# 41 expert blocks with a carried remainder instead of 46, and the out projection one state sooner

## The reference, cut to what matters

```python
x = hidden_states                                   # (4, 512, 128): 2048 tokens, 16 tiles of 128
r = x_n + mamba_block(rmsnorm(layernorm(x)))        # in proj, conv, scan over 16 states, out proj
logits = rmsnorm(r) @ router_w                      # 8 experts
top_w, sel = top_k(softmax(logits), 2)              # two experts for each token
for e in range(8):                                  # FFN = 512
    out += w_e[:, None] * (silu(h @ Wg[e]) * (h @ Wu[e]) @ Wd[e])
# then x += r + out, a gated FFN (384 hidden), attention (16 heads, causal), the same FFN again
```

## Time and profile before

| what | value |
|---|---|
| runs | 688.85 us median of three (685.72 to 689.6) |
| the profiled execution | 688.8 us, its span 687.0 us |
| PE busy | 570.7 us, 83% |
| DVE / ACT / POOL busy | 475.6 / 400.9 / 324.6 us |
| scan stage, first block transposed, block loop, attention | 0 to 276, 276, 278 to 440, 440 to 687 us of the span |
| block loop, mean of one | silu L1353 598 ns, gate times up L1766 688 ns, weights copy L1343 1048 ns |
| indirect DMAs on POOL, mean of one | put L907 976 ns, scatter L899 1008 ns |
| power on POOL, L871 | 1074 ns |

### The profile page before, as it was taken

How to read it: one execution, slowest core, us unless ns; L and a number is a source line. 1 busy time by engine, 2 the same in 40 slices (tenths; PEclk the granted TensorE clock), 3 DMA queues, 4 the chain that set the end, 5 groups by cost and what they waited for, 6 DMA issues and landing times.

```text
span 687.0 us, 11539 instructions
## 1 busy us (share of the span) xinstructions
PE 570.7 (83%) x3652; PEld 379.7 (55%) x3671; DVE 475.6 (69%) x1266; ACT 400.9 (58%) x666; POOL 324.6 (47%) x285
## 2 busy tenths in 40 slices
PE   2967899678677887889989999757799989988887
PEld 1423343224254564879989899625545545544466
DVE  4759997998789987536335653587777878886052
ACT  2677657756755776556756656314356556656731
POOL 5259988895996994225785324412011112112010
PEclk9979999899897999999999999957999999999999
DMA  5845455443755453201152003232003003000001
GB/s 142 305 167 159 150 186 154 143 129 109 241 183 160 142 135 100 68 16 36 54 133 86 20 17 105 68 100 58 9 25 87 10 20 92 4 3 3 1 16 47
DMA packets 49085, 63.32 MB, mean 92 GB/s; under 512 B 7570, under 2 KB 29090, under 8 KB 48770
## 3 DMA queue, kind: packets, MB, share of 16 engines
q1 hardware_dynamic: 43682, 56.65, 27.5%
q0 software_dynamic: 2496, 5.15, 2.1%
q10 hardware_dynamic: 2848, 0.78, 0.5%
HBM read 44.84 MB, written 9.52 MB: 79 GB/s over the span
## 4 chain that ended last, share of the span: by engine, by line
PE 36%; DVE 9%; issue 7%; ACT 4%; POOL 3%; DMA 1%; ACTq 1%; POOLq 0%; another core or an unknown queue 0%; DVEq 0%
PE ps L1792 33%; DVE arena L1712 3%; ACT arena L1296 2%; POOL moe_rows L899 1%; DVE stats L1383 1%; PE ps L2153 1%; DVE x L1647 1%; POOL moe_out L907 1%; DVE nb L1396 1%; ACT r L1296 1%; DMA moe_out<-arena,xT 1%; PE ps L2160 1%; ACT arena L1316 1%; ACT arena L1304 1%; ACTq L1286 1%
## 5 line engine op out<-in xcount | busy, mean ns | idle before, releaser
L1792 PE MATMUL ps<-arena 128*128 128x128 f32 (+11 forms) x2147 | 329.2, 329 | 42.9 <-DVE arena L1712 17.9
L1792 PEld LDWEIGHTS ps<-arena 128*128 128x128 f32 (+2 forms) x2166 | 209.0, 157 | 130.2 <-issue 59.3
L1574 DVE TENSOR_TENSOR_SCAN arena<-ps,arena 128x512 f32<-128x512 f32 x128 | 149.8, 1210 | 21.4 <-ACT ps L1225 15.2
L926 POOL TENSOR_TENSOR arena<-arena 128x1024 f32<-128x1024 f32 x64 | 127.9, 2016 | 25.5 <-DVE arena L1561 19.8
L1792 PE MATMUL ps<-arena,ident 128*128 128x512 f32 x216 | 109.5, 644 | 30.9 <-DVE arena L1586 30.8
L1712 DVE CUSTOM_DVE_ANT_0 arena<-ps,cmask 128x128 f32<-128x128 f32 (+3 forms) x256 | 111.5, 488 | 26.4 <-PE ps L1792 25.2
L1225 ACT ACTIVATE ps<-arena 128x512 f32<-128x512 f32 x128 | 87.4, 689 | 47.2 <-DVE arena L1574 45.5
L1792 PEld LDWEIGHTS ps<-arena,ident 128*128 128x128 f32 x216 | 42.4, 207 | 85.9 <-issue 44.2
L1296 ACT ACTIVATE arena<-ps 128x1024 f32<-128x1024 f32 (+3 forms) x86 | 57.0, 709 | 38.0 <-PE ps L1792 37.6
L907 POOL DMA_INDIRECT moe_out<-arena,xT x46 | 44.9, 976 | 66.5 <-DVE arena L1736 57.1
L1766 DVE TENSOR_TENSOR arena<-arena,ps 128x512 f32<-128x512 f32 x46 | 31.6, 688 | 57.1 <-PE ps L1792 43.6
(11 more groups left out here) (220 smaller groups left out, 700.3 us busy)
## 6 DMA issues: line engine op xcount, KB each, us to landing
arena<-bc_rows SPq DMA_DIRECT2D x118, 256.0 KB, 3.7
arena<-arena SPq DMA_DIRECT2D x64, 64.0 KB
arena<-arena SPq DMA_DIRECT2D x28, 128.0 KB, 2.4
moe_rows<-arena SPq DMA_DIRECT2D x2, 1495.0 KB, 11.8
arena<-moe_rows SPq DMA_DIRECT2D x8, 325.0 KB, 4.3
arena<-in_L_attn_a_Wg SPq DMA_DIRECT2D x8, 256.0 KB, 4.2
arena<-in_L_attn_a_Wu SPq DMA_DIRECT2D x8, 256.0 KB, 4.8
arena<-moe_out SPq DMA_DIRECT2D x4, 512.0 KB, 4.5
```

What stands on the lines that cost most here:

```text
L926: G.tensor_tensor(dBx[:, g % RING, :, :], dx[:, :, cs], bs[:, g % BS, :].unsqueeze(1).to_broadcast([P, CT, L]), ALU.mult).then_inc(s_dbx, 1)
L1574: V.tensor_tensor_scan(hst[:, g % STATES, e, :], bank(6 + e), dBx[:, g % RING, e, :], 0.0, ALU.mult, ALU.add).then_inc(s_scan, 1)
L1792: return T.matmul(o, l, rr, start=start, stop=stop)
```

## The change

The first half gets exactly 16 blocks and the second 25, so 41. Full blocks of each expert come first, then the experts with the largest remainders get one more until 16 are taken; what does not fit goes to one carry block for each of the eight experts, which are the first eight blocks of the second half (expert known beforehand), topped up with tokens of the second half. Outputs of blocks 0 to 23 are stored plainly by SP; outputs of blocks 16 to 40 are scattered by POOL; the first half's outputs are then gathered by 16 indirect DMAs on POOL. Core of the diff (shortened):

```diff
-        NBLK = TH * 2 + NE - 1
+        FIRST = 2 * TH
+        SECOND = (FIRST * P + LEFT + NE * (P - 1)) // P
+        NBLK = FIRST + SECOND
+        assert FIRST * P == 2 * L * HB and LEFT == 256 and SECOND == 25
-        CH = (0, 3, 8, 13, 18, NBLK)
+        CH = ((0, 3, 8, 12, FIRST), (0, 3, 10, 23, SECOND))
...
-   ... first_1 + 2: ("out_proj", 0, 0), 58: ("z", 1, 0), 61: ("z", 1, 1)}
+   ... first_1 + 1: ("out_proj", 0, 0), 58: ("z", 1, 0), 61: ("z", 1, 1)}
-   (30, 1): ("rows", 1, 0), (32, 0): ("abs", 1, 0), ... (34, 0): ("exp", 1, 0), (35, 0): ("log", 1, 0),
-   (36, 0): ("squares", 0, 0), (36, 1): ("squares", 1, 0), (38, 0): ("norm", 0, 0), (38, 1): ("norm", 1, 0),
-   (40, 1): ("input", 0, 0), (41, 0): ("input", 1, 0), (43, 0): ("logits", 0, 0), (45, 0): ("exps", 0, 0),
+   (29, 1): ("rows", 1, 0), (31, 0): ("abs", 1, 0), ... (33, 0): ("exp", 1, 0), (34, 0): ("log", 1, 0),
+   (36, 0): ("squares", 0, 0), (36, 1): ("squares", 0, 1), (37, 0): ("squares", 1, 0), (37, 1): ("squares", 1, 1),
+   (39, 0): ("norm", 0, 0), (39, 1): ("norm", 0, 1), (40, 0): ("norm", 1, 0), (40, 1): ("norm", 1, 1),
+   (41, 1): ("input", 0, 0), (42, 0): ("input", 1, 0), (47, 0): ("exps", 0, 0),
-        DELTA_AT = {4: 1, 30: 2, 36: 3}
+        DELTA_AT = {4: 1, 30: 2, 38: 3}
-   "power": first_1 + 6, "h2turn": first_1 + 7, "router": first_1 + 9,
-   "top_a": first_1 + 11, "top_b": first_1 + 13, "rank": first_1 + 14, "slots": first_1 + 15
+   "power": first_1 + 7, "h2turn": first_1 + 8, "router": first_1 + 10, "top": first_1 + 12,
+   "rank": first_1 + 13, "fill": first_1 + 14, "slots": first_1 + 16, "weights": first_1 + 19
-        SCATTER_FROM = first_1 + 16
+        SCATTER_FROM = first_1 + 17
...
-        in_moe = {0: [("h2norm",)], 2: [("h2turn", 1)], 3: [("route",)], 4: [("top_a",)], 5: [("top_b",)],
-                  6: [("rank",)], 7: [("slots",)], 8: [("add_r", 0)], ...
-                  1: [("h2turn", 0), ("targets", 0)], 22: [("targets", 1)],
-                  27: [("combine", 0), ...], 30: [("combine", 1), ...], ...
+        in_moe = {0: [("h2norm",), ("h2turn", 0)], 1: [("h2turn", 1)], 2: [("route",), ("top",)], 3: [("rank",), ("slots",)],
+                  6: [("exps",)], 8: [("weights",)], 10: [("add_r", 0)], ..., 18: [("targets",)],
+                  28: [("combine", 0), ("f_norm", 0, 0)], 29: [("f_normalise", 0, 0)], 30: [("f_turn", 0, 0), ("f_low", 0, 0)],
+                  33: [("combine", 1), ("f_norm", 0, 1)], 34: [("f_down", 0), ("f_normalise", 0, 1)], 35: [("f_add", 0), ("norm", 0)],
+                  36: [("normalise", 0), ("f_turn", 0, 1), ("f_low", 0, 1)], 37: [("turn", 0)],
+                  38: [("qk", 0, 0)], 39: [("qk_rest", 0, 0), ("qk", 0, 1)], 40: [("qk_rest", 0, 1), ("vals", 0)]}
-        tile_after = {30: (0, 0), 31: (0, 1), 32: (0, 2), 34: (1, 0), 35: (1, 1), 36: (1, 2)}
+        tile_after = {31: (0, 0), 32: (0, 1), 33: (0, 2), 37: (1, 0), 38: (1, 1), 39: (1, 2)}
+        GATHER_AT = (25, 29)
-        LOAD_1, X_FROM = 15, 7
+        LOAD_1, ONES_AT = 12, 22
-        steps, later, use = [], [], []
+        steps, later, use = [("f_down", 1), ("f_add", 1)], [], []
...   # SP, in the block loop
+            for i in range(NBLK):
+                if i == LOAD_1:
+                    load_blocks(1)
+                if i < FIRST + NE:
+                    store_block(i)
...   # POOL: 16 scatters of the second half, clears, then
+            for i in range(FIRST + 1, NBLK):
+                put_block(i - 1)
+                if i == GATHER_AT[0]:
+                    for j in range(TB):
+                        for k in range(2):
+                            gather(0, j, k)
+                if GATHER_AT[1] <= i < GATHER_AT[1] + TB:
+                    for k in range(2):
+                        gather(1, i - GATHER_AT[1], k)
```

More of the change, by code:

```diff
@@ L376, in build @@
         s_yst = [sem(f"block_output_stored{k}") for k in range(YR)]
+        s_ypt = [sem(f"block_output_put{k}") for k in range(YR)]
+        s_nb2 = sem("second_token_numbers")
         s_ga = [sem(f"outputs_gathered{b}") for b in range(NB)]
@@ L440, in o_bank, with half_of, rows_of, stores_before @@
             return 6 if b == NB - 1 and qt % 2 else 7
+        def half_of(i):
+            return (0, i) if i < FIRST else (1, i - FIRST)
+        def rows_of(h, a, b):
+            if h == 0:
+                return xg0[:, a:b, :]
+            return xg1[:, a:b, :] if b <= CH[1][-2] else xg2[:, a - CH[1][-2]:b - CH[1][-2], :]
+        def stores_before(i):
+            return len([n for n in range(min(i, FIRST + NE)) if n % YR == i % YR])
+        def puts_before(i):
+            return len([n for n in range(FIRST, i) if n % YR == i % YR])
+        def expert_of(eng, i):
+            h, k = half_of(i)
+            if h and k < NE:
+                return slice(k, k + 1)
+            if k == (NE if h else 0):
+                eng.wait_ge(s_eb, h + 1)
+            n = k - NE if h else k
+            return bass.ds(eng.value_load(ebt[0:1, h, n:n + 1], min_val=0, max_val=NE - 1), 1)
         def tiles_of(h):
@@ L946, in _ @@
                 scatter(0, j // 2, j % 2)
-            powers(2 * TB, 2 * TB)
+            for b in range(HB, NB):
+                powers(TB * b, TB)
+            pool.wait_ge(s_sc[0], 16 * 2 * TH)
+            ch.link(G.iota(numbers[:, :, D], pattern=[[2 * P, TH]], base=0, channel_multiplier=2,
+                           allow_small_or_imprecise_dtypes=True))
+            G.iota(unused[:, :], pattern=[[1, SECOND]], base=2 * NTOK, channel_multiplier=SECOND,
+                   allow_small_or_imprecise_dtypes=True).then_inc(s_nb2, 1)
             def clear_keys(b):
@@ L1310, in _ @@
             parts = dict(f_turn=f_turn, turn=turn, qk=first_part, vals=vals, place_max=place_max, scores=exps, values=outputs,
-                         h2turn=lambda c: moe_input(HB + c), route=lambda: logits(1), top_a=lambda: router_exp(1))
+                         h2turn=lambda c: moe_input(HB + c), exps=lambda: router_exp(1))
             def tile_silu(n):
@@ L1617, in _ @@
                     count["var"] += 1
-                if g == ROUTE_AT["top_a"]:
-                    top_a(0)
+                if g == ROUTE_AT["top"]:
+                    top(0)
+                if g == ROUTE_AT["fill"]:
+                    fill_blocks(rank_bank(0))
                 if g == ROUTE_AT["slots"]:
-                    find_slots(0, rank_bank(0))
+                    first_slots(rank_bank(0))
+                if g == ROUTE_AT["weights"]:
+                    top_weights(0)
             weigh(NST - 1)
@@ L1728, in _ @@
             parts = dict(norm=norm, normalise=normalise_block, f_norm=f_norm, f_normalise=f_normalise, f_low=f_low, qk_rest=rest_part,
-                         maxima=maxima, o_add=finish, h2norm=lambda: h2_norm(1, asked_h2), top_a=lambda: top_a(1),
-                         top_b=lambda: top_b(1), slots=lambda: find_slots(1, rank_bank(1)), add_r=add_r, combine=combine,
+                         maxima=maxima, o_add=finish, h2norm=lambda: h2_norm(1, asked_h2), top=lambda: top(1),
+                         slots=lambda: second_slots(rank_bank(1)), weights=lambda: top_weights(1), add_r=add_r, combine=combine,
                          targets=targets)
@@ L2224, in _ @@
                 attend(parts, in_moe.get(i, []))
-            down(2 * NBLK - 1, expert[-1])
+            down(NBLK - 1, expert[-1])
             pe.wait_ge(s_hm, NITEM)
```

367 lines of the change are left out of this document (215 added, 152 removed).

## The result

| kernel | median of its runs, us | profiled execution, span, us | mean clock |
|---|---|---|---|
| before | 688.67 (4 runs, 685.72 to 689.60) | 687.0 | 0.944 |
| changed | 697.93 (4 runs, 694.99 to 698.17) | 696.3 | 0.930 |

The changed kernel is slower: ratio 1.0126, 95% interval 1.0092 to 1.0159. The forecast was 683.4, with a range of 670 to 690. I divide both profiles at two places: the first gate product of the block loop on PE, right behind a block transpose, and PE's first product for the maxima.

The account below looks back on a forecast made before the run. PE was taken to bound the block loop, but for gaps, and POOL to set the pace from state 49. From 688.8 us, the loop's -8.8 and the scan stage's +3.4 gave 683.4, range 670 to 690.

Parts of the forecast that it names:

- turn_c and SP's queue: Scan stage: out projection ahead of turn_c releases SP's queue later, so the C row slips and scan(37,0) starts +3.2 us.
- fill_blocks 2.1 us: Routing on DVE in the scan stage: ten operations at some 0.21 us each, 2.1 us together.
- One scatter and product pair fewer lies behind them: End of scan stage: scatters start a state later, leaving one POOL scatter and product pair of 3.22 us fewer behind them.
- The clock in the scan stage: Scan stage: PE's granted clock; the forecast gave it no term in the sum.
- The loop's front, 32.4 us to gate_up(9): Start of block loop: shorter routing route, gate_up(9) starting at 310.4 where it was 313.6, before the scan stage's 3.4 us.
- Block 16's rows: Block loop: second half's rows land at 325.7, PE wants them at 326.2; cost 0, bounds 0 and 1.5 us.
- rival 3: Block loop: second half's routing slow, block 16's rows late, PE stands 11.3 us; 694.7 us in all, chance 0.15.
- combine(0), 3.6 us, and combine(1), 2.5, with 1.0 for slow products: Block loop: PE loses 3.6 and 2.5 us to combines waiting for gathers, plus 1.0 for slow PE after waits.
- The wait ahead of maxima, 5.6: End of block loop: SP's key transfers at 0.645 us each finish late, so maxima waits 5.6 us.
- Rival 1: Block loop: the new waits don't come, as gathers queue faster and keys are placed beside other work; 671.0 us, chance 0.20.
- the loop's -8.8: Whole block loop: maxima starts 8.8 us sooner, at 431.1 instead of 439.9, before the scan stage's slip.

Follow-up runs that it names:

- e2: Changed kernel with only block 0's out projection put back at state 34: 694.0 us, ratio 1.0077 to the kernel before.
- f1: Changed kernel run once more, unedited: 696.5 us, ratio 1.0097 to the kernel before.
- g4: Kernel before with only block 0's out projection one state sooner, on a slower chip: 702.6 us, ratio 1.0036 to the kernel before there.
- e4: Changed kernel with turn_c issued ahead of block 0's out projection: 691.2 us, ratio 1.0013 to the kernel before.
- f2: Changed kernel with fill_blocks moved from state 46 to 48, where POOL stands before its first scatter: 693.4 us, ratio 1.0086 to the kernel before.
- i1: Changed kernel with the 16 gathers replaced by two plain loads, rows not looked up: 684.5 us, ratio 0.9928 to the kernel before.
- h2: Changed kernel with ACT issuing four of k's last eight transfers behind its last silu, slower chip: 716.6 us, ratio 1.0249 to the kernel before there.
- h1: Changed kernel with the gathers replaced by two plain loads, on a slower chip: 698.5 us, ratio 0.9983 to the kernel before there.
- f4: Changed kernel with the keys' ones and zeros placed at block 19 and combine(1) at block 35: 696.1 us, ratio 1.0096 to the kernel before.
- g1: Changed kernel with the gathers replaced by two plain loads, on a slower chip: 698.8 us, ratio 0.9994 to the kernel before there.
- h3: Changed kernel, slower chip: turn_c first, fill_blocks at state 48, weights in loop, ones and zeros at block 19, combine(1) at block 35: 709.9 us, ratio 1.0148.
- i2: Changed kernel: turn_c first, fill_blocks at state 48, weights in loop, ones and zeros at block 19, combine(1) at block 35: 686.6 us, ratio 0.9966.

## Why the prediction was wrong

The first product was to come at 281.4 and came at 288.5. The 7.1 us between lie in three places: 0.9 up to scan(37,0), 4.4 from there to the first scatter (48.4 us, where the sum had 44.0), 1.8 behind it.

- *turn_c and SP's queue*: the right mechanism. scan(37,0) +3.2 forecast, +4.15 in the profile, 2.8 by e2 against f1, +4.4 for the part alone (g4). That 4.15 came near 3.2 is partly luck: the two early waits are in it, and six profiles of the same code without them have +1.2 to +2.7. I did not look at the other order, turn_c first, which turns the loss into a gain of 3 us at scan(37,0) (e4).
- *fill_blocks 2.1 us*: failed. I took its price from a reduction of 0.23, and the reductions take no more than that beside POOL either, though I had allowed for a contended subtraction in `top` (the one in `top_a` takes 1.79 us in the kernel before). It took 5.8, 3.7 more. Away from POOL (f2) it took 2.0, and the first scatter came 2.0 sooner against scan(37,0); the other 1.7 became a wait for POOL. 0.7 of the 4.4 I can't place.
- *"One scatter and product pair fewer lies behind them"*: right. The sum had 58.1 us from the slots to the first product; eleven profiles have 57.7 or 57.8, where the kernel before has 61.0.
- *The clock in the scan stage*: a term that the sum left out. Behind the first scatter it makes 59.9 of 57.7 in the changed kernel's profile; f1, the same kernel, has a loop longer by 2.1 instead. Early in the stage the two long waits, beside a clock of 0.50, go with 1.4 to 3.2 us at scan(37,0).
- *The loop's front, 32.4 us to gate_up(9)*: 32.9 (some 1.5 more in f1, at a lower clock). *Block 16's rows*: in time, no wait; rival 3's mechanism didn't come. The "slower" that it stood for came by another way, which no rival named.
- *combine(0), 3.6 us, and combine(1), 2.5, with 1.0 for slow products*: 7.1 in the sum, 12.3 by i1. This is the largest miss in the loop. The first gather waited for a store that SP issued behind ones and zeros (1.50), the pitch was 1.26 and not 1.17 (my lower bound of 1.06 is in no row; an issue of the earlier trace rows without its gap is 0.96), and the slow products cost 2.6 and 1.7 (2.07 + 3.53 against 1.06 + 1.95, and 4.58 against 2.84) where I took 1.0. No run shows that 1.0, which was my estimate beside a window whose mean clock was 1.00; in its place, after waits of 6.2 and 3.9 us, the granted clock was 0.50 (388.5 to 393.5) and 0.63 (410.7 to 415.3).
- *The wait ahead of maxima, 5.6*: 6.2 on PE. Right, and the cause named has a part in it: h2 moves 4 of SP's transfers and the wait falls by 1.2 against h1.
- *Rival 1*, no new waits, did not come: the loop was 162.1 us, and 149.4 in i1 with the gathers alone gone.

Of the loop's -8.8: front +0.5, the gathers' waits +5.2, the wait ahead of maxima +0.6 are +6.3 of the 9.0 missed. Some 1.4 more is combine(0) itself, which PE feels with no wait too (the step at it is 4.7 us in i1; a block and f_turn make 3.3). 1.3 I can't place.

So the terms that failed are fill_blocks (2.1 us, took 5.8), the gathers' waits with their slow products (7.1 us, took 12.3), and the clock in the scan stage, which was put at nothing (about 2 us behind the scatter, 1.4 to 3.2 ahead of it).

## What to carry to other kernels

When work is moved ahead in an in-order queue, look first at what others wait for behind it, and put that in front (turn_c: scan(37,0) at 173.1 with it in front, at 180.2 behind). Price a small DVE operation with both inputs in arena by what POOL runs beside it: its cost here was the rest of POOL's operation (1.03, 1.98 and 1.34 us for 0.16, 0.22 and 0.17). Moving it away gives back less than it cost if a wait for POOL comes next (2.0 of 3.7 us). Take more than one profile of the same kernel before an edit is given the credit for 3 us. And a chain (gathers, combine, norm, keys) that a shorter loop no longer covers must be shortened with the loop: five blocks, 14 us, went into waits that they had hidden.

## What the runs showed of the hardware

- Three DVE operations that take 0.16 to 0.22 us with POOL idle (f2) took 1.03, 1.98 and 1.34 beside POOL's products of 1.97 us in the changed kernel, and ended with them to within 0.1 us.
- With the same code up to the block loop, eight profiles have its first product between 283.8 and 288.5 us. They differ by where PE's granted clock is low: two (changed, f1) have waits of 2.9 us early in the scan stage, beside a clock of 0.50 in 125 to 135, five (changed, f4, g1, h1, i1) have a clock of 0.50 to 0.67 from 15 to 20 us behind the first scatter (59.9 to 62.1 us to the first product instead of 57.7).
- On two of five chips PE gets through 72 to 76 products in the 19 us of sixteen indirect transfers issued at 1.27 us each (g1, h1, h2, h3), on the others, at 1.28 us, through 156. One kernel won 0.3% on one chip (i2) and lost 1.5% on another (h3).
